# Mixture-of-experts rows: scattered one per choice and summed at the end, or scaled by their gate and added in memory by the scatter

## The reference, cut to what matters

```python
x = L0_attn_x                                   # (8, 1024, 256) float32: 8192 tokens
x = x + _L0_attn_ref(_layernorm(x), ...)        # time mixing and channel mixing
x = x + _L0_ffn_ref(_layernorm(x), expert_sel, keys, values)

def _L0_ffn_ref(x, expert_sel, keys, values):   # 32 experts of 256 -> 128 -> 256
    xt = x.reshape(-1, D)
    gates = jax.nn.sigmoid(jnp.einsum('nd,ed->ne', xt, expert_sel))
    sel_val, sel_idx = jax.lax.top_k(gates, 4)
    gate_full = jnp.zeros_like(gates).at[jnp.arange(N)[:, None], sel_idx].set(sel_val)
    scores = jax.nn.relu(jnp.einsum('nd,edf->nef', xt, keys)) * gate_full[:, :, None]
    return jnp.einsum('nef,efv->nv', scores, values).reshape(B, S, -1)
```

## Time and profile before

| | |
|---|---|
| Timed runs, median (lowest to highest) | 1458.73 us (1451.87 to 1459.62) |
| Profiled execution, span from first to last instruction | 1618.1 us |
| Profiled execution, its own time around the span | not given; only the span is |
| Mean granted TensorE clock in the profiled execution | 0.862 of full speed |
| Busy in the span: PE, DVE, ACT, POOL | 73%, 68%, 42%, 55% |
| HBM read and written | 105.28 MB, 103.71 MB |

### The profile page before, as it was taken

How to read it: one execution, slowest core, us unless ns; L and a number is a source line. 1 busy time by engine, 2 the same in 40 slices (tenths; PEclk the granted TensorE clock), 3 DMA queues, 4 the chain that set the end, 5 groups by cost and what they waited for, 6 DMA issues and landing times. The chain is left out here.

```text
span 1618.1 us, 28319 instructions
## 1 busy us (share of the span) xinstructions
PE 1184.4 (73%) x7399; PEld 1058.3 (65%) x7400; DVE 1096.5 (68%) x2519; ACT 678.8 (42%) x1265; POOL 889.3 (55%) x967
## 2 busy tenths in 40 slices
PE   6799999999999999999881266766776766773000
PEld 5688887888878887788771266666766666673000
DVE  4889898888988889888847444444544444443987
ACT  2555565445654456444443143443443443442000
POOL 1634676666766677667657455555555555554000
PEclk9899999999999999999985588798788788886555
DMA  5000121111111121121163754445444444434998
GB/s 184 14 27 13 68 70 60 66 53 69 65 59 65 46 78 59 61 70 60 54 274 143 249 151 137 140 137 149 133 146 144 133 143 142 141 113 158 390 390 321
DMA packets 101917, 201.25 MB, mean 124 GB/s; under 512 B 16983, under 2 KB 49901, under 8 KB 100464
## 3 DMA queue, kind: packets, MB, share of 16 engines
q1 hardware_dynamic: 63216, 120.34, 23.6%
q0 software_dynamic: 27648, 67.70, 11.5%
q10 hardware_dynamic: 11008, 12.65, 2.2%
HBM read 105.28 MB, written 103.71 MB: 129 GB/s over the span
## 5 line engine op out<-in xcount | busy, mean ns | idle before, releaser
L1359 POOL DMA_INDIRECT expert_rows<-y,dest x320 | 320.4, 1001 | 257.1 <-issue 224.9
L1124 POOL DMA_INDIRECT lists<-rows,slot x256 | 276.5, 1080 | 73.3 <-issue 70.4
L1269 PE MATMUL ps<-xt_hi,keys 128*128 128x256 f32 x640 | 180.0, 341 | 114.0 <-issue 110.1
L1336 DVE TENSOR_TENSOR xt_lo<-ps,xt_hi 128x512 fp32r<-128x512 f32 x160 | 110.5, 690 | 186.0 <-ACT xt_hi L1296 107.6
L1269 PEld LDWEIGHTS ps<-xt_hi,keys 128*128 128x128 f32 x640 | 131.4, 226 | 130.7 <-issue 129.5
L1308 ACT ACTIVATE y<-ps 128x512 f32<-128x512 f32 x160 | 96.1, 601 | 130.2 <-PE ps L1284 113.2
L535 PE MATMUL ps<-wv_hi,k_hi 128*128 128x256 f32 x512 | 149.6, 292 | 0.0
L537 PE MATMUL ps<-wv_lo,k_hi 128*128 128x256 f32 x512 | 147.8, 289 | 0.9 <-issue 0.9
L539 PE MATMUL ps<-wv_hi,k_lo 128*128 128x256 f32 x512 | 147.6, 288 | 0.3 <-issue 0.3
L1296 ACT ACTIVATE xt_hi<-ps 128x512 fp32r<-128x512 f32 x160 | 96.6, 604 | 122.0 <-PE ps L1256 101.9
L1282 PE MATMUL ps<-experts_w,h_hi 128*128 x320 | 108.4, 339 | 47.6 <-DVE h_lo L1343 36.7
(11 more groups left out here) (201 smaller groups left out, 3544.4 us busy)
## 6 DMA issues: line engine op xcount, KB each, us to landing
xr<-lists SPq DMA_DIRECT2D x160, 260.0 KB
ye<-expert_rows SPq DMA_DIRECT2D x32, 1024.0 KB, 8.1
x_sb<-in_x SPq DMA_DIRECT2D x16, 512.0 KB, 3.8
residual<-xp SPq DMA_DIRECT2D x16, 512.0 KB, 4.9
experts_raw<-in_expert_in SPq DMA_DIRECT2D x8, 1024.0 KB, 15.1
lists<-zeros SPq DMA_DIRECT2D x25, 260.0 KB, 10.8
expert_rows<-y,dest POOLq DMA_INDIRECT x320
resid<-residual SPq DMA_DIRECT2D x20, 256.0 KB, 5.4
```

The lines of the kernel that those rows point to most:

```text
L1124: pool.indirect_dma_start(lists, bass.IndirectOffsetOnAxis(ap=slot[:, q, n:n + 1], axis=0), rows[:, q, n // TOPK, :], None).then_inc(scatt ...
L1269: mm = pe.matmul(ps[:, H + q, 0:BLOCK], keys[:, (r - 1) % SLOTS, half, k * DE:(k + 1) * DE], m[:, q, k, :], start=n == 0, stop=n == 3 * KD ...
L1336: dve.tensor_tensor(xt_lo[:, q].rearrange("p k b -> p (k b)"), ps[:, XT + q, :], xt_hi[:, q].rearrange("p k b -> p (k b)").bitcast(F32), A ...
L1359: pool.indirect_dma_start(expert_rows, bass.IndirectOffsetOnAxis(ap=dest[:, r, s:s + 1], axis=0), y[:, r, s, :], None, bounds_check=OUT_RO ...
```

## The change

A token row in `lists` now carries four gates, one number in which the four experts are packed (5 bits each) and the token's number, and no longer four row numbers. In the expert stage VectorE unpacks the experts, compares them with the block's expert and multiplies by the gates; the sum over the four is the row's gate. `dest` is the token's number plus the offset of one of two accumulators: even blocks add to the first, odd ones to the second. ScalarE scales y by the gate while it copies it, in two halves. The scatter adds its rows to the accumulator (`compute_op=ALU.add`) and has no bounds check: padding goes to 256 spare rows behind each accumulator, a row of another expert adds zero. Before the scatters of block i GpSimd waits until both of block i-2 have landed. The residual is stored into the first accumulator in the mixing stage; the second is filled with zeros there, two stores of 256 KB per tile by SP. The last stage has 16 steps of 512 tokens: two loads, one addition, one store.

```diff
-ROW = D + TOPK
+GATE, OWNERS, TOKEN = D, D + TOPK, D + TOPK + 1
+ROW = TOKEN + 1
...
+SUMS = 2
+SUM_ROWS = N + BLOCK
...
                 if has_v:
                     after(sp, x1_ready, t - 1)
-                    sp.dma_start(residual[bass.ds((t - 2) * TILE, TILE), :]
+                    sp.dma_start(sums[bass.ds((t - 2) * TILE, TILE), :]
                                  .rearrange("(j p) d -> p j d", p=P), xp[:, p]).then_inc(x1_stored[p], 16)
+                    for n in range(1, SUMS):
+                        for h in range(TILE // BLOCK):
+                            clear((t - 2) * TILE + (n * SUM_ROWS + h * BLOCK))
...
-                dve.tensor_copy(gates[:, bass.ds(V * J, J), :], top8[:, :, 0:TOPK])
+                dve.tensor_copy(rows[:, p, :, GATE:GATE + TOPK], top8[:, :, 0:TOPK])
                 after_route(4)
                 dve.tensor_copy(expert[:], top8_at[:, :, 0:TOPK]).then_inc(route_step, 1)
-                after_route(5)
-
-                dve.scalar_tensor_tensor(rows[:, p, :, D:ROW], expert[:], float(SPACED), out_row[:],
-                                         ALU.mult, ALU.add).then_inc(route_step, 1)
+                dve.tensor_copy(rows[:, p, :, TOKEN], token[:]).then_inc(route_step, 1)
                 after_route(6)
-                dve.tensor_scalar(out_row[:], out_row[:], float(TILE * TOPK), None, ALU.add)
+                dve.tensor_scalar(token[:], token[:], float(TILE), None, ALU.add)
+                dve.tensor_tensor(weighted[:], expert[:], weights[:].unsqueeze(1).broadcast_to([P, J, TOPK]),
+                                  ALU.mult).then_inc(route_step, 1)
+                after_route(7)
+                dve.tensor_reduce(packed[:], weighted[:], AX_X, ALU.add).then_inc(route_step, 1)
...
+                dve.tensor_copy(rows[:, p, :, OWNERS].bitcast(I32), packed[:])
...
                     after(act, sent[b], 16 * SUB * (ring - 1 if r >= 2 else ring - 2) + 16 * SUB)
-                    act.activation(y[:, b].rearrange("p s d -> p (s d)"), ps[:, Y + q, :],
-                                   ACT.Copy).then_inc(ycopy_ready, 1)
+                    act.wait_ge(dest_ready, i - 2 + 1)
+                    for n in range(SUB):
+                        ins = act.activation(y[:, b, n, :], ps[:, Y + q, n * D:(n + 1) * D], ACT.Copy,
+                                             scale=gate[:, b, n:n + 1])
+                    ins.then_inc(ycopy_ready, 1)
...
             def step(i, r, ring):
+                before = r - SUMS
+                if before >= 0:
+                    pool.wait_ge(sent[before], 16 * SUB * (ring + 1))
+                elif not isinstance(ring, int):
+                    settled_on(pool, sent[before], 16 * SUB * ring)
                 settled_on(pool, ycopy_ready, i + 1, dest_ready)
                 for s in range(SUB):
                     pool.indirect_dma_start(
-                        expert_rows, bass.IndirectOffsetOnAxis(ap=dest[:, r, s:s + 1], axis=0), y[:, r, s, :],
-                        None, bounds_check=OUT_ROWS - 1, oob_is_err=False).then_inc(sent[r], 16)
+                        sums, bass.IndirectOffsetOnAxis(ap=dest[:, r, s:s + 1], axis=0), y[:, r, s, :],
+                        None, compute_op=ALU.add).then_inc(sent[r], 16)
...
+            for t in range(NT):
+                r = t % DEPTH
+                after(sp, stored[r], 16 * (t // DEPTH))
+                for n in range(SUMS):
+                    row = n * SUM_ROWS + t * TILE
+                    sp.dma_start(part[:, r, n, :], sums[row:row + TILE, :].rearrange("(p j) d -> p (j d)", p=P)
+                                 ).then_inc(loaded[r], 16)
...
+                dve.wait_ge(loaded[r], 16 * SUMS * (t // DEPTH + 1))
+                dve.tensor_tensor(part[:, r, 0, :], part[:, r, 0, :], part[:, r, 1, :], ALU.add
+                                  ).then_inc(added, 1)
...
+                act.wait_ge(added, t + 1)
+                act.dma_start(out[t * TILE:(t + 1) * TILE, :].rearrange("(p j) d -> p (j d)", p=P),
+                              part[:, r, 0, :]).then_inc(stored[r], 16)
```

More of the change, by code:

```diff
@@ L86, in program @@
         consts = keep("consts", [P, C_END])
-        gates = keep("gates", [P, N // P, TOPK])
         list_end = keep("list_end", [P, E])
@@ L90, in program @@
         full = keep("full", [P, E])
-        zeros = keep("zeros", [P, SUB * ROW])
+        padding = keep("padding", [P, SUB, ROW])
         ones_bf = keep("ones_bf", [P, P], BF16)
@@ L323, in fill @@
             eng.dma_start(lists[bass.ds(row, BLOCK), :].rearrange("(p s) c -> p (s c)", p=P),
-                          zeros[:]).then_inc(filled, 16)
+                          padding[:].rearrange("p s c -> p (s c)")).then_inc(filled, 16)
         eng.wait_ge(filled, 16 * E)
@@ L337, in _, with clear @@
                 sp.dma_start(to, g[source]).then_inc(loaded[name], 16)
-            sp.wait_ge(setup_v, 1)
-            for row in range(OVERFLOW, LIST_ROWS, BLOCK):
+            sp.wait_ge(padding_ready, 1)
+            for row in (EMPTY, *range(OVERFLOW, LIST_ROWS, BLOCK)):
                 sp.dma_start(lists[row:row + BLOCK, :].rearrange("(p s) c -> p (s c)", p=P),
-                             zeros[:]).then_inc(area_cleared, 16)
+                             padding[:].rearrange("p s c -> p (s c)")).then_inc(area_cleared, 16)
+            def clear(row):
+                sp.dma_start(sums[bass.ds(row, BLOCK), :].rearrange("(p s) d -> p s d", p=P),
+                             padding[:, :, 0:D]).then_inc(sums_cleared, 16)
+            for n in range(SUMS):
+                clear(n * SUM_ROWS + N)
             def step(t, p, pair):
@@ L764, in step @@
                     dve.memset(ones_f[:], 1.0)
-                    dve.memset(zeros[:], 0.0).then_inc(setup_v, 1)
+                    dve.memset(padding[:], 0.0).then_inc(setup_v, 1)
+                    dve.wait_ge(setup_v, 1)
                     dve.wait_ge(x_loaded[0], 16)
@@ L1196, in expert_phase @@
     mark = sb("mark", [P, SUB, TOPK])
+    shifted, owner = (sb(name, [P, SUB, TOPK], I32) for name in ("shifted", "owner"))
+    owner_bit = sb("owner_bit", [P, TOPK], I32)
+    gate = sb("block_gate", [P, RING, SUB])
     dest = sb("dest", [P, RING, SUB], U32)
@@ L1315, in _ @@
             expert = {}
+            owner_step, owner_bits_ready = sem("owner_step"), sem("owner_bits_ready")
+            for k in range(TOPK):
+                ins = dve.memset(owner_bit[:, k:k + 1], BITS * k)
+            ins.then_inc(owner_bits_ready, 1)
+            dve.wait_ge(owner_bits_ready, 1)
             def load_expert(i, r):
@@ L1346, in step @@
                 if a_block:
-                    after(dve, sent[r], 16 * SUB * ring)
                     dve.wait_ge(mark_ready, i + 1)
-                    dve.tensor_reduce(dest[:, r, :], mark[:], AX_X, ALU.min,
-                                      apply_absolute_value=True).then_inc(dest_ready, 1)
+                    dve.tensor_reduce(gate[:, r, :], mark[:], AX_X, ALU.add).then_inc(dest_ready, 1)
             loop(dve, step, drain=1)
@@ L1368, in combine_phase @@
 def combine_phase(nc, scope, sem, g):
-    gates, expert_rows, residual, out = g["gates"], g["expert_rows"], g["residual"], g["out"]
-    GROUPS = 2
-    STEPS = N // P // GROUPS
+    sums, out = g["expert_rows"], g["out"]
     DEPTH = 4
-    ye = scope.enter_context(nc.sbuf_tensor("ye", [P, DEPTH, GROUPS, TOPK, D], F32))
-    resid = scope.enter_context(nc.sbuf_tensor("resid", [P, DEPTH, GROUPS, D], F32))
-    ye_loaded = [sem(f"ye_loaded_{r}") for r in range(DEPTH)]
-    stored = [sem(f"stored_{r}") for r in range(DEPTH)]
@@ L1377, in combine_phase @@
[L1377 to L1397 removed]
+    part = scope.enter_context(nc.sbuf_tensor("part", [P, DEPTH, SUMS, J * D], F32))
@@ L1399, in _ @@
+    loaded = [sem(f"part_loaded_{r}") for r in range(DEPTH)]
+    stored = [sem(f"out_stored_{r}") for r in range(DEPTH)]
+    added = sem("added")
+    with nc.Block() as block:
         @block.sync
         def _(sp):
-            def step(i, r, ring, head):
-                tokens = GROUPS * P
-                after(sp, sum_step, ADDS * (i - DEPTH + 1))
-                sp.dma_start(ye[:, r], expert_rows[bass.ds(i * (tokens * TOPK), tokens * TOPK), :]
-                             .rearrange("(g p k) d -> p g k d", p=P, k=TOPK)).then_inc(ye_loaded[r], 16)
-                if not head:
-                    after(sp, stored[r], 16 * ring)
-                    sp.dma_start(resid[:, r], residual[bass.ds(i * tokens, tokens), :]
-                                 .rearrange("(g p) d -> p g d", p=P)).then_inc(resid_loaded[r], 16)
@@ L1429, in _ @@
-            loop(dve, step)
+            for t in range(NT):
+                r = t % DEPTH
+                dve.wait_ge(loaded[r], 16 * SUMS * (t // DEPTH + 1))
+                dve.tensor_tensor(part[:, r, 0, :], part[:, r, 0, :], part[:, r, 1, :], ALU.add
+                                  ).then_inc(added, 1)
         @block.scalar
```

(12 more changed lines are left out.)

103 lines of the change are left out of this document (46 added, 57 removed).

## The result

The changed kernel takes **1601.95 us** (median of 4 runs, 1598.73 to 1605.51) where the kernel before took 1457.06 us beside it (4 runs, 1451.87 to 1459.62): ratio 1.1015, interval 1.099 to 1.1041. It is 10% slower; the forecast was 1406 us, with a range of 1388 to 1510.

A forecast was written before the change was run, and what follows sets the result against it. The prediction took POOL, at about 2.58 us per block, to bound the timed kernel. Terms -56 + 2 + 0 + 0 + 0 + 1 = -53 us took the 1458.7 us median to 1406 us, range 1388 to 1510.

The forecast's parts named there:

- up to the first scatter: Mixing stage: extra zero stores hidden, small VectorE operations bare only in the last tile; +2 us, +8 if cover is gone.
- last scatter to first load: End of the expert stage: the last landing comes later by what adding costs in landing time; +1 us.
- Expert stage, POOL: Expert stage: still two scatters per block, each adding scatter taken at the plain form's 0.99 us; 0 us.
- The sign named for a wrong forecast: Expert stage blocks in busy runs more than 2.9 us apart, or a last stage moving less than 330 GB/s.
- POOL's own time grows: Expert stage rival: describing adding rows makes the 0.99 us grow by half; +157 us, total 1563 us; chance 0.16.
- The new wait: Expert stage: waiting for block i-2's scatters stays hidden in POOL's pace, 3.7 + X against 5.16 us per two blocks; 0.
- X: Extra landing time of an adding scatter over a plain one, taken near 1 us; the wait decides from 1.5 us on.
- the rival: Expert stage: the landing takes POOL's place as bound; 1545 us at X of 3.2 us; chance 0.18 beyond break-even.
- The estimate from its latency: Expert stage: HBM access of 0.2 to 2 us taken as X, costing 0 to 40 us, total 1406 to 1446.
- Last stage: Last stage: fewer bytes at 389 GB/s, 73.7 us in place of 129.6; -56 us.
- VectorE: Expert stage: dependent small operations add 0.6 us per block, about 2.25 us busy, under POOL's 2.58; cost 0.
- these stalls: Expert stage: late y from ScalarE, some 147 us, nearly the 159.4 us taken to occur only in the profiled execution.

The follow-up runs named there:

- e1b: Changed kernel with the scatter writing its rows instead of adding them, on a chip where the kernel before takes 1453.31 us: 1404.2 us, ratio 0.9652.
- b2_before: The kernel before, unchanged, profiled on a chip of the first kind (kernel before about 1455 us there, 1617 to 1631 on the second kind): 1452.73 us, ratio 0.9993.
- e8_one_sum_plain: Changed kernel with one accumulator, each block waiting for the one before, and plain writing scatters instead of adding: 1763.07 us, ratio 1.0816.
- Experiments 4: Runs on the landing wait: changed kernel with four accumulators (1608.35 us), one accumulator adding (2039.86 us) and one accumulator with plain writes (1763.07 us).
- after: Profile of the changed kernel itself, on a chip of the first kind: span 1603.7 us, timed median 1601.95 us.
- e6b_bf16_rows: The kernel before with expert result rows kept as bfloat16 in memory, on a chip where the kernel before takes 1452.35 us: 1443.08 us, ratio 0.9935.
- before: Profile of the kernel before that the prediction read, on a chip of the second kind: span 1618.1 us.
- e6_bf16_rows: The kernel before with expert result rows kept as bfloat16 in memory, on a chip of the second kind: 1615.9 us, ratio 0.9905.
- e1_plain_write: Changed kernel with the scatter writing its rows instead of adding them, on a chip where the kernel before takes 1617.37 us: 1573.8 us, ratio 0.9729.
- e5_plain_half: Changed kernel with plain writing scatters of 64 rows instead of adding ones of 128: 1588.86 us, ratio 0.9822.
- e4_half_rows: Changed kernel with adding scatters of 64 rows instead of 128, still two per block: 1561.72 us, ratio 0.9654.
- e3_four_sums: Changed kernel with four accumulators instead of two, so block i waits for block i-4: 1608.35 us, ratio 0.9941.
- a2_after_again: The changed kernel, unaltered, repeated on a chip where the kernel before takes 1630.89 us: 1624.9 us, ratio 0.9963.
- e7_one_sum: Changed kernel with one accumulator, adding, so every block waits for the landing of the one before: 2039.86 us, ratio 1.2514.
- e9_eight_more: The kernel before with eight extra unused one-column matmuls per block on TensorE: 1630.77 us against 1455.57, ratio 1.1189.
- e10_one_pass: The kernel before with one matmul instead of three for each expert-stage product: 1454.7 us against 1455.57, ratio 0.9991.

## Why the prediction was wrong, point by point

By the spans of the two profiles on chips of the first kind, 1603.7 - 1450.3 = +153.4 us:

| term | forecast | changed kernel | plain form (e1b) |
|---|---|---|---|
| up to the first scatter (905.7) | +2 | +5.2 | +0.9 |
| first to last scatter (413.0) | 0 | +200.9 | +5.7 |
| last scatter to first load (4.3) | +1 | +2.5 | +0.3 |
| last stage (127.3) | -56 | -55.2 | -54.9 |
| sum | -53 | +153.4 | -48.0 |

In brackets the us of `b2_before`.

- **The step that failed is the term "Expert stage, POOL": "I take 0.99, the form with the same 1 KB rows".** It measured 1.557 us. Times 320, less 0.985: 183 us of the 196 that the forecast lacks. The sign named for a wrong forecast, blocks more than 2.9 us apart, came with it: 3.85. I had bounded it by 0.99 and the 1.08 us of the other scatter, two plain forms that differ in row length. Such rows bound a change of length, not of kind; the trace of before had nothing of this kind, and the upper bound was no bound.
- The rival "POOL's own time grows" had the right place, POOL's duration, and was given 0.16. Its size, half of 0.99, was 0.08 us short per scatter, and it gave 1563 us for 1602. Its sign was the one seen: POOL's mean duration. Its reason, more to describe per row, is only in part borne out: by the estimate above 0.41 of the 0.59 us don't grow with the rows, and the price doesn't follow the bytes of the plain form. What POOL does in that time no run shows. "Against: nothing in the trace" was true and should have weighed more: a rival that nothing speaks against, on the engine that binds, deserves more than one chance in six.
- The Trainium skill (Collectives: The Full Stack, the stop on SDMA and CCE) draws two reads and one write for an adding step, and pointed to this rival. The runs agree on the side; they don't show that share.
- The new wait was put at 0, and came out at 10 to 16 us, but by luck. I took the last bytes at 2.3 us for the landing and 0.1 us to wake POOL; `b2_before` has a median landing of 2.9 us and `e8_one_sum_plain` 3.60 from start to next start. At the forecast pace two blocks would then take 1.29 + 3.60 + X = 4.9 + X against 5.16: the wait decides from X = 0.3 us on, not 1.5, and the measured 0.5 lies above that, by this estimate some 16 us. It was hidden because POOL itself became slower (7.4 us for 6.5). Nor do the "2.7 us" and "1.1 to 1.2 us more" of the rival fit its own threshold; 5.16 - 1.29 - 0.99 is 2.9, and 1.6 more.
- In the plain form, where the wait is tighter, landings end 36.3 us of idleness. But all idle time ahead of its scatters is only 10.9 us more than in `b2_before` (127.2 for 116.3), while its scatters are busy 5.0 us less (311.8 for 316.8): what the wait and the work added on VectorE and ScalarE cost there together is near 11 us, not 0.
- The Trainium skill (DMA: Bandwidth & Descriptors, Rules for kernel authors) gave the reason for the wait; no run here leaves it out. The estimate from its latency, X of 0.2 to 2 us, holds the measured 0.5; that this X is such an access no run shows, and the threshold under the 40 us was the wrong one.
- A term was missing: what adding rows cost the DMA engines, 3.3 us per block as an estimate (Experiments 4). With POOL's price right it changes nothing, but with POOL at 0.99 the forecast would still not have held.
- Last stage: 72.1 us for 73.7 forecast; right. VectorE: shifted, owner, mark and dest take 0.16, 0.17, 0.23 and 0.17 us in the changed kernel; in `e1b_plain_write` it is busy 298 of 370 us, 2.1 us per block for 2.25 forecast, and not the bound. ScalarE: two halves, 0.84 us for 0.78.
- "I take these stalls as belonging to the profiled execution": wrong, they belong to some chips. What was built on it, POOL as the bound at 2.58 us per block, was right for the chips of the timed runs (2.59).

## What to carry to other kernels

Price first what the change does to the instruction that binds, even where only an argument of it changes: here 320 instructions at 0.57 us more took back three times what halving the last stage's transfers gained. If the trace shows no instruction of that kind, rows of another kind did not bound it here, and the rival that nothing spoke against was the one that came. Price it on both sides, the engine that issues and the DMA engines that carry it out. And where a profile is longer than the timed runs, take a second profile before a sum is made against either.

## What the runs showed of the hardware

- An adding indirect scatter of 128 rows of 1 KB costs GpSimd 1.557 us (`after`), a plain one 0.960 to 0.985 (`e1b_plain_write`, `b2_before`), and 0.984 with rows of 512 bytes (`e6b_bf16_rows`). A landing takes a median of 4.0 us from its issue (`after`) for 2.9 (`b2_before`).
- The adding form goes out in smaller packets. The queue's rows (packets, MB, share), of the changed kernel:

```profile
q0 software_dynamic: 58368, 76.32, 28.1%
```

  and of `e1b_plain_write`:

```profile
q0 software_dynamic: 27648, 76.32, 14.9%
```

  The same recorded bytes in 30720 packets more, 96 per scatter. With half the rows a plain scatter has 16 packets fewer (27648 - 22528, over 320), an adding one 64 (58368 - 37888, over 320): a packet for four rows of 1 KB, and one for each row. The DMA engines' share rises with it, 0.85 at 138 GB/s against 0.66 at 205. The profile records 80.44 MB read from memory with the adding and without it, so a read of the row that is added to stands in none of its figures.
- On the chips of the second kind (profiles `before`, `e6_bf16_rows`, `e1_plain_write` and `e5_plain_half`) TensorE's results reach the next engine up to 5 us late, in fits; in the kernel before these stand some 17.6 us apart. In `e5_plain_half` ScalarE stood idle for 5.23 us before it took transposes that had ended at 1193.4 us, at 1199.26. In these four a block took 3.50 to 3.60 us. In `e8_one_sum_plain` (4.83) it is weaker: 19 results are taken 0.7 to 0.9 us after their recorded end between 1000 and 1300 us. In the same stretch it is absent in `e4_half_rows` (3.46), `e3_four_sums` (3.75), `a2_after_again` (3.82) and `e7_one_sum` (6.56), and on the chips of the first kind in every profile, down to 2.59. So the pace of the blocks alone does not explain it; its cause stays open.
- In `e9_eight_more`, with TensorE busy all the time, f32 matmuls of one column, each with its own weight load (recorded at 192 ns), stand 0.115 us apart, and those of 256 columns 0.12. Each call of one column is recorded as two of them.
- In `e10_one_pass` a mean granted clock of 0.61 costs nothing, with a third of the products' matmuls left and POOL as the bound.
